# TensorE's loop body turned by part of a tile, and its code aligned to blocks of 256 instructions, in a linear-attention layer

## Chip, core and metric

One Trainium2 chip, one core of it. The metric is the device time of one execution in microseconds (us), as the median of runs; smaller is better.

## What is computed

A layer with causal linear attention and a feed-forward part, on x of 8 sequences x 2048 positions x 512 values, 16 heads of 32, in float32:

```python
q = split_heads(x @ Wq.T + bq); k = split_heads(x @ Wk.T + bk); v = split_heads(x @ Wv.T + bv)
q, k = exp(q), exp(k)
kv = cumsum(k[:, :, :, None] * v[:, :, None, :], axis=1)
k1 = cumsum(k, axis=1)
num = einsum('zsD,zsDd->zsd', q, kv)
den = sum(q * k1, axis=-1, keepdims=True)
x = layernorm(x + merge_heads(num / den) @ Wo.T + bo)
x = layernorm(x + tanh(x @ weight @ aux_weight1 @ aux_weight2 + bias))
```

## The kernel before

The work is cut into 128 tiles of 128 positions, tile n being positions 128 (n // 8) onward of sequence n % 8. For a tile the kernel works out the scores within it, masks them, multiplies by V ("attend"), adds what a running state of the earlier tiles gives, divides by the denominators, projects with Wo, normalises, and multiplies by Wf, the product of the three feed-forward matrices, made once at the start.

Each engine has its own program, written out by hand, and they meet only by semaphores. The unit is `slot(c, k)`, the work of one step, k from 0 to 7 in a chunk of 8 tiles. `run_slots` (L213) writes the first slots out, then a loop of 13 iterations of 8 slots (`nc.Fori`, L219, with `hint_back_edge=True`), then the last slots. The first and last slots know their number when the program is built (`c.static()`); those in the loop compare semaphores with registers that five instructions set at the top of each iteration (L181 to L183). The loop's branch is a compare-and-branch at the end, and a hint instruction at the top names it.

On TensorE a slot has two parts. Small matmuls, five groups of 16 float32 instructions, which the chip runs as 32 weight loads and 32 matmuls each: denominators of tile k-1 (L368), the state's share of its numerator (L372), scores of tile k (L425), attend of k-1 (L381), the state's update by k-2 (L436). Then large ones, of 12 weight loads and 12 matmuls with 512 columns each: Q's and K's projections for tile k+4, V's for k, the output projection of k-1 and the feed-forward of k-2, all by `three_pass` (L309; its three matmuls are L312, L313, L314). A load and a matmul are an instruction each. Waits on semaphores are carried by a load or, where there is more than one, stand as instructions of their own: 13 in a slot (two before the denominators, three before scores, one before attend, two before Q, one before K, two before the output projection, two before the feed-forward). A slot so is 453 instructions: 13 and 440 loads and matmuls. With the hint, five register instructions, the addition and the branch the loop's body is 3632.

The other engines' parts (ScalarE evicts and exponentiates, VectorE scans, divides and normalises, GpSimd masks and splits in two parts, SyncE loads and stores) are not touched.

Of the kernel before, what the change touches and what calls it, by code (L numbers as in the profile page):

```python
# [26 lines left out]
def linear_attention_ffn_kernel(nc, x, wqT, wkT, wvT, woT, bq, bk, bv, bo, w, a1T, a2, bf, out):  # L27
# [5 lines left out]
    P = 128  # L33
    B, S, D = x.shape
    NK = D // P
    HD = 32
    HG = P // HD
    QUAD = 4
    NI = S // P
    NT = NI * B  # L40
# [16 lines left out]
    with ctx:  # L57
# [106 lines left out]
        def wait(engine, semaphore, value):  # L164

            if not isinstance(value, int) or value > 0:
                engine.wait_ge(semaphore, value)

        def wait_before(engine, *waits):

            engine.wait_ge(mhalf_ready, 1)
            for semaphore, value in waits:
                wait(engine, semaphore, value)
# [134 lines left out]
        def _(pe):  # L308
# [37 lines left out]
                pe.wait_ge(c_ready, 1)  # L346
                pe.wait_ge(consts_ready, 1)

            def slot(c, k):
                b = k % QUAD  # L350
                s = (k // QUAD) % 2
                ns = 1 - s
                cols = slice(b * P, (b + 1) * P)
                att = c.exists(k)
                prev = c.exists(k - 1)
                ffn = c.exists(k - 2)
                proj = c.exists(k + 4)
                heads = [(g, j, slice(g * HD, (g + 1) * HD), slice(j * HD, (j + 1) * HD))
                         for g in range(NK) for j in range(HG)]

                def denominators(n):

                    ts, tcols = (n // QUAD) % 2, slice(n % QUAD * P, (n % QUAD + 1) * P)

                    wait_before(pe, (qk1_ready, c.count(n + 1)), (o_ready, c.count(n)),
                                (state_ready, c.state_count(n - 1)))
                    for g, j, quarter, h in heads:
                        last = nc.tensor.matmul(den_ps[quarter, j, :], ones[h, :], qk1[h, g, :], start=True, stop=True)  # L368
                    last.then_inc(den_done, 1)
                    if c.reads_state(n):  # L370
                        for g, j, quarter, h in heads:
                            nc.tensor.matmul(num_ps[quarter, j, :], state[h, n % B, g, :], QT[h, ts, g, tcols],  # L372
                                             start=True, stop=False, skip_group_check=True)

                def attend(n):
                    wait(pe, v_ready, c.count(n + 1))
                    wait(pe, masked, c.count(n + 1))
                    for j in range(HG):
                        for g in range(NK):
                            f0 = g * P + j * HD  # L380
                            last = nc.tensor.matmul(num_ps[g * HD:(g + 1) * HD, j, :], V[:, n % 2, f0:f0 + HD],  # L381
                                                    A[:, n % 2, j, g, :], start=not c.reads_state(n),
                                                    stop=True, skip_group_check=True)
                    last.then_inc(num_done, 1)

                def output_projection():
                    if not ffn:
                        pe.wait_ge(woh_ready, 1)
                        pe.wait_ge(wol_ready, 1)
                    wait(pe, oh_ready, c.count(k))  # L390
                    wait(pe, ol_ready, c.count(k))

                    if att:
                        wait(pe, scores_out[3], c.count(k + 1))
                    wait(pe, r_ready, c.count(k - 1))
                    three_pass(oproj_ps, lambda f: oH[:, f, :], lambda f: oL[:, f, :],
                               lambda f: WoH[:, f, :], lambda f: WoL[:, f, :]).then_inc(oproj_done, 1)

                def feed_forward():
                    wait(pe, x1h_ready, c.count(k - 1))  # L400
                    wait(pe, x1l_ready, c.count(k - 1))

                    if proj:
                        wait(pe, q_ready, c.count(k + 5))
                    elif att:
                        wait(pe, scores_out[0], c.count(k + 1))
                    wait(pe, z_ready, c.count(k - 2))
                    three_pass(ffn_ps, lambda f: x1H[:, f, :], lambda f: x1L[:, f, :],
                               lambda f: WfH[:, f, :], lambda f: WfL[:, f, :]).then_inc(ffn_done, 1)

                if att and prev:
                    denominators(k - 1)
                if att:
                    wait(pe, k_ready, c.quad_count(k))
                    wait(pe, q_ready, c.quad_count(k))

                    wait(pe, z_ready, c.count(k - 2))
                    wait(pe, k_ready, c.count(k + 4))
                    wait(pe, v_ready, c.count(k))  # L420
                    wait(pe, r_ready, c.count(k - 1))
                    if not prev:
                        pe.wait_ge(c_ready, 1)
                    for g, j, _, h in heads:
                        last = nc.tensor.matmul(SC[:, j, g * P:(g + 1) * P], KT[h, s, g, cols],  # L425
                                                QT[h, s, g, cols], start=True, stop=True)
                    last.then_inc(scores_done, 1)
                if att and prev:
                    attend(k - 1)
                if c.updates_state(k - 2):  # L430
                    n = k - 2
                    wait(pe, ktok_loaded[n % B], c.part_count(n))
                    for g in range(NK):
                        for j in range(HG):
                            f0 = g * P + j * HD
                            last = nc.tensor.matmul(state_ps[j * HD:(j + 1) * HD, g * HD:(g + 1) * HD],  # L436
                                                    Ktok[:, j * P + g * HD:j * P + (g + 1) * HD],
                                                    V[:, n % 2, f0:f0 + HD], start=True, stop=True)
                    last.then_inc(state_done, 1)
                if proj:  # L440
                    if not c.exists(k + 3):
                        pe.wait_ge(wqh_ready, 1)
                        pe.wait_ge(wql_ready, 1)
                    wait(pe, xh_ready, c.quad_count(k + 4))
                    wait(pe, xl_ready, c.quad_count(k + 4))

                    if att:
                        wait(pe, scores_out[0], c.count(k + 1))
                    wait(pe, q_ready, c.count(k + 4))
                    three_pass(qproj_ps, lambda f: WqH[:, f, b * P:(b + 1) * P],  # L450
                               lambda f: WqL[:, f, b * P:(b + 1) * P], lambda f: xTH[:, ns, f, :],
                               lambda f: xTL[:, ns, f, :]).then_inc(qproj_done, 1)
                    if not c.exists(k + 3):
                        pe.wait_ge(wkh_ready, 1)
                        pe.wait_ge(wkl_ready, 1)
                    if att:
                        wait(pe, scores_out[1], c.count(k + 1))
                    wait(pe, k_ready, c.count(k + 4))
                    three_pass(kproj_ps, lambda f: WkH[:, f, b * P:(b + 1) * P],
                               lambda f: WkL[:, f, b * P:(b + 1) * P], lambda f: xTH[:, ns, f, :],  # L460
                               lambda f: xTL[:, ns, f, :]).then_inc(kproj_done, 1)
                if att:
                    if not prev:
                        pe.wait_ge(wvh_ready, 1)
                        pe.wait_ge(wvl_ready, 1)
                    wait(pe, scores_out[2], c.count(k + 1))
                    three_pass(v_ps, lambda f: xTH[:, s, f, cols], lambda f: xTL[:, s, f, cols],
                               lambda f: WvH[:, f, :], lambda f: WvL[:, f, :]).then_inc(v_done, 1)
                if att and not c.exists(k + 1):
                    denominators(k)  # L470
                    attend(k)
                if prev:
                    output_projection()
                if ffn:
                    feed_forward()

            run_slots(pe, slot, 8, 2, {-3: multiply_aux, -2: multiply_weight, -1: multiply_bv})

        @block.scalar
        def _(act):  # L480
# [355 lines left out]
```

## Time and profile before

| what | value |
|---|---|
| median of 3 runs | 2352.6 us (2350.2 to 2352.68) |
| the profiled execution's own time | 2354.96 us |
| its span, first to last instruction | 2353.2 us |
| granted TensorE clock, mean | 0.991 |
| TensorE busy (matmuls) | 2250.8 us, 96% |
| TensorE weight loads | 1833.2 us, 78% |
| VectorE, GpSimd, ScalarE busy | 1620.6, 1289.1, 1012.5 us |
| instruction queue q8 | 235 packets, 3.85 MB |

### The profile page before, as it was taken

The page shows a single profiled execution, that of the slowest core. Times are in us where ns is not written, and L with a number is a line of the kernel's source. Part 1 is how long each engine was busy: PE and PEld are TensorE (multiplying, and loading weights), DVE is VectorE, ACT ScalarE, POOL GpSimd, SP SyncE. Part 2 cuts the span into 40 slices and gives each one's busy share as a digit, 9 for nine tenths or more (in the row PEclk, how much of TensorE's full clock was granted, in tenths as well). Part 3 has the DMA queues.
Part 4 walks back from the last instruction along what each step waited for, and adds up shares of the span by engine and source line. Part 5 has one row for each costly group of instructions (what it writes and reads, how often), then busy time and mean ns, then how long its engine had stood idle before and what let it go on. Part 6 is the DMA issues. An engine that isn't in the chain of part 4 may idle for free.

```text
span 2353.2 us, 71216 instructions
## 1 busy us (share of the span) xinstructions
PE 2250.8 (96%) x27784; PEld 1833.2 (78%) x27784; DVE 1620.6 (69%) x2444; ACT 1012.5 (43%) x1683; POOL 1289.1 (55%) x1797
## 2 busy tenths in 40 slices
PE   3999999999999999999999999999999999999985
PEld 2778887878888888887878788787888878788864
DVE  3477776776776767767767767677777677677674
ACT  2344444444444444444444444444444444444442
POOL 1255555556555555555555555555555655555553
PEclk9999999999999999999999999999999999999997
DMA  5133333333333333333333333333333333333221
GB/s 156 46 101 107 108 108 107 104 108 109 105 110 103 109 109 104 109 108 100 113 105 105 105 107 109 104 105 107 110 104 109 109 100 107 111 101 113 69 68 55
DMA packets 294453, 242.74 MB, mean 103 GB/s; under 512 B 33329, under 2 KB 225841, under 8 KB 294193
## 3 DMA queue, kind: packets, MB, share of 16 engines
q1 hardware_dynamic: 294192, 238.69, 32.5%
q8 instruction: 235, 3.85, 0.7%
q14 instruction: 26, 0.20, 0.0%
HBM read 139.99 MB, written 98.57 MB: 101 GB/s over the span
## 4 chain that ended last, share of the span: by engine, by line
PE 94%; issue 2%; DVE 2%; ACT 1%; DMA 1%; POOL 1%; SPq 0%; POOLq 0%; DVEq 0%; ACTq 0%
PE SC L312 26%; PE SC L313 25%; PE SC L314 24%; PE SC L425 6%; PE ND L381 5%; PE ND L372 3%; PE ND L368 2%; PE ND L436 2%; DVE o L670 0%; PE ND L312 0%; PE ND L313 0%; PE ND L314 0%; DMA KT<-wkT 0%; DMA QT<-wqT 0%; ACT A L552 0%
## 5 line engine op out<-in xcount | busy, mean ns | idle before, releaser
L756 POOL TENSOR_SCALAR_AFFINE_SELECT A<-A 128x512 f32<-128x512 f32 x512 | 327.8, 674 | 313.2 <-ACT A L552 313.1
L670 DVE RECIPROCAL o<-ND 128x512 f32<-128x512 f32 x128 | 427.8, 3342 | 1.1 <-PE ND L381 0.9
L727 DVE TENSOR_TENSOR xres<-SC,xres 128x512 f32<-128x512 f32 x128 | 88.6, 692 | 457.0 <-PE SC L314 456.8
L750 POOL TENSOR_TENSOR oL<-o,oH 128x512 fp32r<-128x512 f32 x128 | 166.1, 1298 | 324.8 <-ACT oH L531 324.8
L542 ACT ACTIVATE WK<-xres,shift,rstd 128x512 f32<-128x512 f32 x128 | 104.4, 816 | 530.4 <-POOL shift L796 530.4
L552 ACT ACTIVATE A<-SC 128x512 f32<-128x512 f32 x512 | 264.7, 603 | 48.7 <-PE SC L425 48.6
L312 PE MATMUL SC<-xTH,WqH 128*128 128x512 f32 x512 | 211.3, 413 | 31.4 <-POOL xTL L785 27.3
L785 POOL TENSOR_TENSOR xTL<-xin,xTH 128x512 fp32r<-128x512 f32 x128 | 165.7, 1295 | 100.8 <-ACT xTH L580 100.7
L312 PE MATMUL SC<-WfH,x1H 128*128 128x512 f32 x512 | 201.4, 393 | 14.4 <-issue 7.8
L683 DVE TENSOR_TENSOR_SCAN WK<-ones,k,KT 128x128 f32<-128x128 f32 x512 | 207.7, 468 | 9.9 <-PE ND L368 9.9
L313 PE MATMUL SC<-xTL,WqH 128*128 128x512 f32 x512 | 201.2, 393 | 13.0 <-issue 13.0
L557 ACT ACTIVATE QT<-SC,bcol 128x512 f32<-128x512 f32 x128 | 88.4, 691 | 289.8 <-PE SC L314 289.8
L312 PE MATMUL SC<-WoH,oH 128*128 128x512 f32 x512 | 201.0, 393 | 9.8 <-issue 7.8
L312 PE MATMUL SC<-xTH,WkH 128*128 128x512 f32 x512 | 200.3, 391 | 7.7 <-DVE WkL L616 7.7
L312 PE MATMUL SC<-WvH,xTH 128*128 128x512 f32 x512 | 199.6, 390 | 2.7 <-ACT A L552 2.7
L314 PE MATMUL SC<-xTH,WqL 128*128 128x512 f32 x512 | 201.4, 393 | 0.0
L313 PE MATMUL SC<-WfL,x1H 128*128 128x512 f32 x512 | 200.8, 392 | 0.0
L314 PE MATMUL SC<-WfH,x1L 128*128 128x512 f32 x512 | 200.5, 392 | 0.0
L314 PE MATMUL SC<-WoH,oL 128*128 128x512 f32 x512 | 200.4, 391 | 0.0
L313 PE MATMUL SC<-WoL,oH 128*128 128x512 f32 x512 | 200.2, 391 | 0.0
L313 PE MATMUL SC<-xTL,WkH 128*128 128x512 f32 x512 | 200.0, 391 | 0.0
L314 PE MATMUL SC<-xTH,WkL 128*128 128x512 f32 x512 | 199.9, 390 | 0.0
(100 smaller groups left out, 5025.0 us busy)
## 6 DMA issues: line engine op xcount, KB each, us to landing
xin<-x SPq DMA_DIRECT2D x512, 64.0 KB, 1.8
xres<-x SPq DMA_DIRECT2D x128, 256.0 KB, 2.6
x_rows<-WK SPq DMA_DIRECT2D x128, 256.0 KB, 2.9
WK<-x_rows SPq DMA_DIRECT2D x512, 64.0 KB, 2.0
out<-WK SPq DMA_DIRECT2D x128, 256.0 KB, 2.1
k_rows<-WK SPq DMA_DIRECT2D x120, 256.0 KB, 2.0
WK<-k_rows SPq DMA_DIRECT2D x480, 64.0 KB, 1.9
QT<-wqT SPq DMA_DIRECT2D x4, 256.0 KB, 4.5
```

Of the source, the lines that this page charges most:

```text
L312: nc.tensor.matmul(out, statH(k), movH(k), start=(k == 0), stop=False)
L313: nc.tensor.matmul(out, statH(k), movL(k), start=False, stop=False)
L314: last = nc.tensor.matmul(out, statL(k), movH(k), start=False, stop=(k == NK - 1))
L381: last = nc.tensor.matmul(num_ps[g * HD:(g + 1) * HD, j, :], V[:, n % 2, f0:f0 + HD], A[:, n % 2, j, g, :], start=not c.reads_state(n), st ...
L425: last = nc.tensor.matmul(SC[:, j, g * P:(g + 1) * P], KT[h, s, g, cols], QT[h, s, g, cols], start=True, stop=True)
L542: nc.scalar.activation(x1[:, n % 2, :], xres[:, n % 2, :], ACT.Identity, bias=shift[:, 0:1], scale=rstd[:, 0:1]).then_inc(x1_ready, 1)
L552: nc.scalar.activation(A[:, k % 2, j, :, :].rearrange("p g q -> p (g q)"), SC[:, j, :], ACT.Copy).then_inc(scores_out[j], 1)
L670: nc.vector.reciprocal(o[:, :, :], den_ps).then_inc(recip_ready, 1)
L683: last = nc.vector.tensor_tensor_scan(qk1[:, g, :], ones[:, 0:1].to_broadcast([P, P]), KT[:, s, g, cols], k1[:, k % B, g:g + 1], ALU.mult, ...
L750: nc.gpsimd.tensor_tensor(oL[:, :, :], o[:, :, :], oH[:, :, :].bitcast(F32), ALU.subtract).then_inc(ol_ready, 1)
L756: last = nc.gpsimd.affine_select(out=A[:, k % 2, j, :, :], in_=A[:, k % 2, j, :, :], compare_op=ALU.is_ge, fill=0.0, base=0, pattern=[[0, ...
L785: nc.gpsimd.tensor_tensor(halves[1], xin[:, m % XIN, :].rearrange("p (t g q) -> p g t q", t=HG, q=HD), halves[0].bitcast(F32), ALU.subtrac ...
```

## The change

`slot` is cut in two: `small(c, k)` with the small matmuls and `large(c, k)` with the projections. The order of all matmuls stays as it was. What moves is the place where the loop begins and ends: an iteration was small(0), large(0), ..., small(7), large(7), and is now large(0), small(1), large(1), ..., large(7), small(8), with the first `small` in front of the loop. Two directives on the places of instructions are new. `head_slot={pe.engine: 160}` puts the loop's first instruction at place 160 of a block of 256. `addr_align(256, offset=0, max_nops=255)` in front of V's projection fills up with no-operation instructions until V's first load is the first of a block: 39 behind the loop's head (160 + 57 instructions = 217), and 59 in the seven other tiles (453 + 59 = 512). It is written in the loop alone. The last alignment is followed by 404 instructions, the branch among them, so the loop ends 148 instructions into a block.

```diff
+            def small(c, k):
...
                 if att and prev:
-                    denominators(k - 1)
+                    denominators(c, k - 1)
...
+            def large(c, k):
...
+                if not c.static():
+
+                    pe.addr_align(256, offset=0, max_nops=255)
                 if att:
                     if not prev:
                         pe.wait_ge(wvh_ready, 1)
...
-            run_slots(pe, slot, 8, 2, {-3: multiply_aux, -2: multiply_weight, -1: multiply_bv})
+            setup = {-3: multiply_aux, -2: multiply_weight, -1: multiply_bv}
+            for t in range(-8, B):
+                small(Chunk(t // B), t % B)
+                large(Chunk(t // B), t % B)
+                if t in setup:
+                    setup[t]()
+
+            small(Chunk(1), 0)
+            with nc.Fori(1, NI - 2, engines=(pe.engine,), hint_back_edge=True, head_slot={pe.engine: 160}) as it:
+                c = Chunk(it, pe)
+                for k in range(B):
+                    large(c, k)
+                    small(c, k + 1)
+            for t in range(NT - 2 * B, NT + 2):
+                if t > NT - 2 * B:
+                    small(Chunk(t // B), t % B)
+                large(Chunk(t // B), t % B)
```

On TensorE, the loop's head in the kernel before, from the entry on (ISA rows are the register instructions):

```order
L219 UNCONDITIONAL_BRANCH
L219 BRANCH_PREFETCH_HINT
L219 ISA
L181 ISA x3
L183 ISA
L368 MATMUL ND<-WK,ones 32x128 x16
L372 MATMUL ND<-QT,state 32x128 x16
L425 MATMUL SC<-QT,KT 128x128 x16
L381 MATMUL ND<-A,V 32x128 x16
L436 MATMUL ND<-V,WK 32x32 x16
L312 MATMUL SC<-xTH,WqH 128x512
```

and in the changed kernel, where the small matmuls have other line numbers (L359, L363, L398, L372 and L409 for L368, L372, L425, L381 and L436), and the ISA row of L498 ahead of the branch is the directive for place 160:

```order
L372 MATMUL ND<-A,V 32x128 x16
L409 MATMUL ND<-V,WK 32x32 x16
L498 ISA
L498 UNCONDITIONAL_BRANCH
L498 BRANCH_PREFETCH_HINT
L498 ISA
L181 ISA x3
L183 ISA
L312 MATMUL SC<-xTH,WqH 128x512
L313 MATMUL SC<-xTL,WqH 128x512
```

The five small groups have gone in front of the loop, and Q's projection is what follows the registers. The loop's end on TensorE in the kernel before:

```order
L312 MATMUL SC<-WfH,x1H 128x512
L313 MATMUL SC<-WfL,x1H 128x512
L314 MATMUL SC<-WfH,x1L 128x512
L219 REGISTER_ALU
L219 COMPARE_AND_BRANCH
```

and in the changed kernel:

```order
L314 MATMUL SC<-WfH,x1L 128x512
L359 MATMUL ND<-WK,ones 32x128 x16
L363 MATMUL ND<-QT,state 32x128 x16
L398 MATMUL SC<-QT,KT 128x128 x16
L372 MATMUL ND<-A,V 32x128 x16
L409 MATMUL ND<-V,WK 32x32 x16
L498 REGISTER_ALU
L498 COMPARE_AND_BRANCH
```

The branch stood behind the feed-forward's long matmuls and now stands behind the state's update. The seam between K's and V's projection on TensorE in the changed kernel:

```order
L313 MATMUL SC<-xTL,WkH 128x512
L314 MATMUL SC<-xTH,WkL 128x512
L474 ISA
L312 MATMUL SC<-WvH,xTH 128x512
L313 MATMUL SC<-WvL,xTH 128x512
```

The ISA row is the directive that becomes 39 or 59 no-operations; in the kernel before the row of WkL is followed by that of WvH at once.

## Rows read from the trace of the kernel before

**Rows 1.** The page: busy times, and the chain that ended last.

```profile
PE 2250.8 (96%) x27784; PEld 1833.2 (78%) x27784; DVE 1620.6 (69%) x2444; ACT 1012.5 (43%) x1683; POOL 1289.1 (55%) x1797
PE 94%; issue 2%; DVE 2%; ACT 1%; DMA 1%; POOL 1%; SPq 0%; POOLq 0%; DVEq 0%; ACTq 0%
PE SC L312 26%; PE SC L313 25%; PE SC L314 24%; PE SC L425 6%; PE ND L381 5%; PE ND L372 3%; PE ND L368 2%; PE ND L436 2%; DVE o L670 0%; PE ND L312 0%; PE ND L313 0%; PE ND L314 0%; DMA KT<-wkT 0%; DMA QT<-wqT 0%; ACT A L552 0%
```

**Rows 2.** Waits of TensorE in 219:2038.5: total us, times, longest us.

```profile
PE SC L313 <- issue: 13.0, 12, 1.5
PE ND L436 <- issue: 2.7, 9, 0.4
PE ND L372 <- issue: 1.5, 5, 0.4
```

**Rows 3.** Timeline of weight loads behind one return: start us, us, instruction, [idle before].

```profile
1059.51 0.23 PEld L368 LDWEIGHTS ND<-WK,ones 32*32 32x32 f32 x32 [0.35 <-issue]
1059.64 0.43 PEld L372 LDWEIGHTS ND<-QT,state 32*32 32x32 f32 x5
1060.78 0.23 PEld L372 LDWEIGHTS ND<-QT,state 32*32 32x32 f32 x27 [0.70 <-issue]
...
1063.73 0.19 PEld L313 LDWEIGHTS SC<-xTL,WqH 128*128 128x128 f32 x1
1065.36 0.19 PEld L314 LDWEIGHTS SC<-xTH,WqL 128*128 128x128 f32 x1 [1.44 <-issue]
...
1078.86 0.23 PEld L368 LDWEIGHTS ND<-WK,ones 32*32 32x32 f32 x32 [0.35 <-issue]
```

**Rows 4.** Queue q8 in 1057.3:1057.5, 1062.9:1063.0, 1066.8:1066.9 and 1056:1196: packets, MB, share.

```profile
q8 instruction: 1, 0.02, 61.2%
q8 instruction: 1, 0.02, 60.0%
q8 instruction: 1, 0.02, 77.2%
q8 instruction: 15, 0.25, 0.8%
```

**Rows 5.** The same timeline in the iteration before that.

```profile
920.64 0.23 PEld L372 LDWEIGHTS ND<-QT,state 32*32 32x32 f32 x27 [0.29 <-issue]
...
924.67 0.19 PEld L314 LDWEIGHTS SC<-xTH,WqL 128*128 128x128 f32 x1 [0.89 <-issue]
```

**Rows 6.** Timelines of a clean tile: weight loads, Q's first matmul, the next tile's start.

```profile
1096.10 0.23 PEld L368 LDWEIGHTS ND<-WK,ones 32*32 32x32 f32 x32 [0.35 <-issue]
1096.24 0.66 PEld L372 LDWEIGHTS ND<-QT,state 32*32 32x32 f32 x32
1097.10 0.99 PEld L425 LDWEIGHTS SC<-QT,KT 32*128 32x128 f32 x32 [0.20 <-issue]
1098.21 0.81 PEld L381 LDWEIGHTS ND<-A,V 128*32 128x32 f32 x32
...
1099.55 0.47 PE L312 MATMUL SC<-xTH,WqH 128*128 128x512 f32 x1
...
1113.32 0.23 PEld L368 LDWEIGHTS ND<-WK,ones 32*32 32x32 f32 x32 [0.35 <-issue]
```

**Rows 7.** Timeline of weight loads: first tile of the loop, first tile behind it.

```profile
222.35 0.23 PEld L368 LDWEIGHTS ND<-WK,ones 32*32 32x32 f32 x32 [0.35 <-issue]
...
2041.51 0.18 PEld L368 LDWEIGHTS ND<-WK,ones 32*32 32x32 f32 x16 [0.35 <-issue]
2042.25 0.16 PEld L368 LDWEIGHTS ND<-WK,ones 32*32 32x32 f32 x13 [0.56 <-issue]
```

**Rows 8.** Queue q8 in 2038.5:2040.5, behind the loop's end.

```profile
q8 instruction: 1, 0.02, 3.0%
```

**Rows 9.** Timeline of matmuls: three gaps of the last tiles.

```profile
2261.38 0.47 PE L312 MATMUL SC<-WoH,oH 128*128 128x512 f32 x1 [2.60 <-issue]
2278.15 0.47 PE L312 MATMUL SC<-WoH,oH 128*128 128x512 f32 x1 [2.60 <-issue]
2293.51 0.76 PE L312 MATMUL SC<-WoH,oH 128*128 128x512 f32 x1 [2.60 <-issue]
```

**Rows 10.** Windows around them: us, PE busy (instructions), granted clock, DMA share, GB/s.

```profile
2262.60:2266.00 3.40, 3.40 (x10) 0.51 0.22 82
...
2275.40:2278.20 2.80, 0.20 (x2) 1.00 0.36 103
2278.20:2285.00 6.80, 6.79 (x88) 1.00 0.10 39
...
2293.40:2296.80 3.40, 3.29 (x8) 0.50 0.00 0
```

More of the change, by code:

```diff
@@ L347, in multiply_bv, with denominators @@
                 pe.wait_ge(consts_ready, 1)
-            def slot(c, k):
+            heads = [(g, j, slice(g * HD, (g + 1) * HD), slice(j * HD, (j + 1) * HD))
+                     for g in range(NK) for j in range(HG)]
+            def denominators(c, n):
+                ts, tcols = (n // QUAD) % 2, slice(n % QUAD * P, (n % QUAD + 1) * P)
+                wait_before(pe, (qk1_ready, c.count(n + 1)), (o_ready, c.count(n)),
+                            (state_ready, c.state_count(n - 1)))
+                for g, j, quarter, h in heads:
+                    last = nc.tensor.matmul(den_ps[quarter, j, :], ones[h, :], qk1[h, g, :], start=True, stop=True)
+                last.then_inc(den_done, 1)
+                if c.reads_state(n):
+                    for g, j, quarter, h in heads:
+                        nc.tensor.matmul(num_ps[quarter, j, :], state[h, n % B, g, :], QT[h, ts, g, tcols],
+                                         start=True, stop=False, skip_group_check=True)
@@ new lines, in attend @@
+            def attend(c, n):
+                wait(pe, v_ready, c.count(n + 1))
+                wait(pe, masked, c.count(n + 1))
+                for j in range(HG):
+                    for g in range(NK):
+                        f0 = g * P + j * HD
+                        last = nc.tensor.matmul(num_ps[g * HD:(g + 1) * HD, j, :], V[:, n % 2, f0:f0 + HD],
+                                                A[:, n % 2, j, g, :], start=not c.reads_state(n),
+                                                stop=True, skip_group_check=True)
+                last.then_inc(num_done, 1)
@@ new lines, in small @@
+            def small(c, k):
+                s = (k // QUAD) % 2
+                cols = slice(k % QUAD * P, (k % QUAD + 1) * P)
+                att = c.exists(k)
+                prev = c.exists(k - 1)
+                if att and prev:
+                    denominators(c, k - 1)
+                if att:
+                    wait(pe, k_ready, c.quad_count(k))
+                    wait(pe, q_ready, c.quad_count(k))
+                    wait(pe, z_ready, c.count(k - 2))
+                    wait(pe, k_ready, c.count(k + 4))
+                    wait(pe, v_ready, c.count(k))
+                    wait(pe, r_ready, c.count(k - 1))
+                    if not prev:
+                        pe.wait_ge(c_ready, 1)
+                    for g, j, _, h in heads:
+                        last = nc.tensor.matmul(SC[:, j, g * P:(g + 1) * P], KT[h, s, g, cols],
+                                                QT[h, s, g, cols], start=True, stop=True)
+                    last.then_inc(scores_done, 1)
+                if att and prev:
+                    attend(c, k - 1)
+                if c.updates_state(k - 2):
+                    n = k - 2
+                    wait(pe, ktok_loaded[n % B], c.part_count(n))
+                    for g in range(NK):
+                        for j in range(HG):
+                            f0 = g * P + j * HD
+                            last = nc.tensor.matmul(state_ps[j * HD:(j + 1) * HD, g * HD:(g + 1) * HD],
+                                                    Ktok[:, j * P + g * HD:j * P + (g + 1) * HD],
+                                                    V[:, n % 2, f0:f0 + HD], start=True, stop=True)
+                    last.then_inc(state_done, 1)
@@ L357, in slot @@
                 proj = c.exists(k + 4)
[L358 to L384, printed above, removed]
                 def output_projection():
@@ L409, in feed_forward @@
                                lambda f: WfH[:, f, :], lambda f: WfL[:, f, :]).then_inc(ffn_done, 1)
-                if att and prev:
-                    denominators(k - 1)
[L414 to L439, printed above, removed]
                 if proj:
@@ L469, in slot @@
                 if att and not c.exists(k + 1):
-                    denominators(k)
-                    attend(k)
+                    denominators(c, k)
+                    attend(c, k)
                 if prev:
```

## Prediction

> **What bounds the kernel now.** I read the page first. TensorE is busy 96% of the span and is 94% of the chain that ended last, nearly all on the three lines of the projections and the five of the small matmuls [rows 1]. VectorE, the next, is at 69%. So time comes and goes only as TensorE's stream gets denser or thinner. Next I asked what TensorE waited for in the stretch of the loop, 219 to 2038.5 us. It waits for no other engine there: all its idle time ends with "issue", 12 times before L313, up to 1.5 us each, and 14 shorter ones before L436 and L372 [rows 2]. The reader is to see that the tile's data is always there and that something in the delivery of instructions is late, about once for each of the 12 returns to the loop's head.
>
> Then the timeline of the weight loads around one return. The five small groups start at 1059.51; the fifth load of L372 is followed by 0.70 us of nothing (resumed 1060.78), and the second load of the Q projection by 1.44 us (resumed 1065.36) [rows 3]. I counted the instructions between the two resumptions, each float32 matmul of 16 being 32 loads and 32 matmuls, and each further wait an instruction of its own: the matmul of the fifth load 1, the other 27 pairs 54, three semaphore waits 3, scores 64, one wait 1, attend 64, state 64, two waits 2, the first pair of Q 2, the next load 1. That is 256, the number that the change aligns to. The instruction queue q8 began one packet of 0.02 MB in 1057.3 to 1057.5, one in 1062.9 to 1063.0 and one in 1066.8 to 1066.9, and 15 in the whole iteration [rows 4], whose body is 3632 instructions (14.2 blocks). So a block is asked for when the one ahead of it is entered, one block ahead only, and takes 1065.36 - 1060.78 = **4.58 us** to be usable; in another iteration 924.67 - 920.64 = 4.03 us [rows 5]. It shows only where 256 instructions run out faster, and a tile's 320 small ones take 3.45 us (1096.10 to 1099.55 in a clean tile, whose 60 large matmuls have the other 13.8 us, 0.23 us each) [rows 6]. The Trainium skill ("Runtime: NRT & Kernel Launch", Instruction fetch mechanics) says that crossing a 16 KiB boundary is mostly hidden; by that the change would have nothing to win. The row of 1.44 us differs, and decides.
>
> **What alignment removes.** A clean tile lasts 1113.32 - 1096.10 = 17.22 us, or 17.24 us; the first tile of this iteration 1078.86 - 1059.51 = 19.35 us [rows 3, 6]. From the first L368 load of the loop (222.35) to the one behind it (2041.51) are 1819.16 us for 104 tiles [rows 7]. At 17.23 us they would be 1791.9 us: **27 us** is all that late blocks cost in the loop. In the new order a tile is 453 instructions and a pad of 59, so two blocks: V, O and FFN, 36 pairs at 0.23 us (8.3 us), are in front of the small ones, and the next boundary falls 47 instructions into scores; behind it are some 2.2 us of small ones and 5.5 us of Q and K. Both stretches exceed 4.58 us. I take the whole 27 us as gone.
>
 In the kernel before that request comes a whole projection phase ahead of the branch. In the new one it comes in scores. The sequencer has just waited there, so it enters the last block between the first load of scores (1097.10) and the moment the array reaches that instruction, 47/64 of 1.11 us later (1097.9); I take 1097.3. Small matmuls end and Q begins at 1099.55 [rows 6]. The request takes between 3.8 us (1.4 us from the resumption at 1065.36 to the next packet, and 2.4 us from the packet begun at 1062.9 to 1063.0 to its use at 1065.36) [rows 3, 4] and 4.58 us; I take 4.2, between them. Behind the jump come the branch, the hint, five register instructions and two waits before Q's first load. No row prices those; three waits before scores leave 0.30 us (0.20 idle and a load's 0.10) [rows 6], so 0.10 each, about 1.0 us in all. They were free before, under the queued FFN; behind the small matmuls nothing is queued. Q then starts at 1097.3 + 4.2 + 1.0 = 1102.5 instead of 1099.55: **+2.95 us** at each of 12 returns, 35 us. Bounds: 1097.3 + 3.8 + 0.8 gives +2.35 (28 us), 1097.9 + 4.58 + 1.0 gives +3.9 (47 us). The Trainium skill, same section, says that a branch to a target outside the two pages held forces a fetch before execution goes on; with the measured 4 us it speaks against the new place, and the trace agrees as to the exit.
>
> The next block after the jump (V's) is asked for at the jump and needed 1.0 + 24 x 0.23 = 6.5 us later: hidden. Entering the loop costs one such jump, 0 to 3 us; the tiles outside the loop stay unaligned, and those behind it will meet their boundaries at other places than before (0.56 us at the exit is one). I take +1 us for both, within -2 to +4.
>
> **The clock.** Each return leaves TensorE idle for about 3 us. Three gaps of that size stand in the tail: 2.60 us idle before 2261.38, and two like it; the granted clock was then 0.51 for 3.4 us (2262.6 to 2266.0) and 0.50 (2293.4 to 2296.8), and stayed 1.00 after the one at 2275.4 [rows 9, 10]. That is 2.4 GHz down to 1.2, and costs 1.7 us each time. In the loop the array was busier before the gap than there, so I count half of 12 returns: +10 us, bounds 0 and 20 us.
>
> **What the pads cost.** 91 pads of 59 instructions and 13 of 39 stand between K's last matmul and V's first. They hide if they end within the sequencer's lead. That lead from rows: after the jump the packet of the following block began at 1057.3 to 1057.5, a request precedes its packet by 1.4 us (above), and the array came to the first small load at 1059.51 [rows 3, 4]: 3.5 us. So up to 3.5/59 = 59 ns each costs nothing. Below, a load or matmul passes in 3.6 ns (L368: 64 in 0.23 us) [rows 6]; above, a semaphore wait takes 0.10 us. No row shows a pad. It waits for nothing and sets nothing, so I put it under the wait, at 59 ns or less, and price 0. At 0.10 us it is (5.9 - 3.5) x 91 = +218 us. The Trainium skill ("TensorE: Matmul & The Clock Gate", Wait — 56ns, not 53.3ns?) gives about 62 ns for a matmul decoded in software; were a pad the same, the sum would be +14 us more.
>
> **Sum.** -27 + 35 + 1 + 10 = +19 us. The profiled execution took 2354.96 us beside its span of 2353.2, 2.4 us above the median of 2352.6, so the forecast is 2352.6 + 19 to 21: **2373 us**. Its own range is -27 + 28 - 2 = -1 to -27 + 47 + 4 + 20 = +44: 2352 to 2397.
>
> **Rivals.**
> - *The head is there in time* (faster). If it is asked for earlier than at entry to the last block, or is kept, only the 1.0 us of branch, registers and waits shows: -27 + 12 + 1 = -14 us, 2339; with these hidden too, 2326. It decides once a return costs under 27/12 = 2.25 us, and my low bound is 2.35. For it: the branch of before shows no idle time. Against it: 15 packets an iteration, one for each block, so nothing is kept, and the exit.
> - *The pads show* (slower). V's matmuls start late in every tile by 59 times the pad's price less 3.5 us. From 59 ns up, each 10 ns adds 54 us; at 0.07 to 0.10 us the time is 2430 to 2590. For it: every instruction of the sequencer that a row shows costs 0.10 us. Against it: a pad has nothing to wait for.
> - *The change doesn't do what it says.* If the blocks don't begin where the padding assumes, the stalls of before remain at other tiles, and the new loop end is cheap or dear by luck: about 2353.
>
> **How the numbers follow.** Return stall with hidden pads 0.43, of which 0.03 within 0.2% (4.7 us, about what a measurement of this kernel can tell from no change); head in time 0.27, nearly all faster; pads show 0.24; no effect 0.06, split mostly into the same. Faster 0.28, same 0.08, slower 0.64. The range takes the likeliest case, the faster one and the lower edge of the pads: 2328 to 2440 us. The likeliest one's own is 2352 to 2397.
>
> **What would show it.** Right: no idle time at L372 and L313 in the loop, clean tiles of 17.2 us, seven in eight; one gap of about 3 us before the first L312 of Q at each of 12 returns; 17 q8 packets an iteration; some short stretches at half clock behind the gaps. If the pads show, the gap stands before the first L312 of V (WvH) in each tile. I am wrong if the gap before Q is under 2 us, or if tiles stay at 19 us somewhere in the body.

## The result, and the profile after

The changed kernel takes **2416.95 us** (median of 6 runs, 2412.0 to 2420.73) against 2352.41 us of the kernel before on the same chip (6 runs, 2350.2 to 2352.68): ratio 1.0278, 95% interval 1.0264 to 1.0292. It is 64.5 us slower, where +21 us was forecast. The direction held. The wide range, 2328 to 2440 us, held too, because it took in the lower edge of the rival "The pads show"; the range of the likeliest case alone, 2352 to 2397 us, did not. Most of the excess is one term.

The page of the changed kernel, lines that answer to [rows 1], and the groups of the first matmul of Q's and of V's projection (busy us, mean ns of one, idle time before them). The last line is V's group in the kernel before:

```profile
PE 2277.1 (94%) x27752; PEld 1832.2 (76%) x27752; DVE 1613.9 (67%) x2444; ACT 1010.8 (42%) x1683; POOL 1287.4 (53%) x1797
q8 instruction: 261, 4.28, 0.9%
PE 92%; issue 3%; DVE 2%; ACT 1%; DMA 1%; POOL 1%; SPq 0%; POOLq 0%; DVEq 0%; ACTq 0%
L312 PE MATMUL SC<-xTH,WqH 128*128 128x512 f32 x512 | 215.0, 420 | 67.4 <-issue 36.3
L312 PE MATMUL SC<-WvH,xTH 128*128 128x512 f32 x512 | 207.0, 404 | 21.7 <-issue 19.0
L312 PE MATMUL SC<-WvH,xTH 128*128 128x512 f32 x512 | 199.6, 390 | 2.7 <-ACT A L552 2.7
```

TensorE still bounds the kernel. "issue" rose from 2% to 3% of the chain, and V's projection, which had no wait that ended with "issue" before, has 19.0 us of them. The loop's waits of TensorE (219 to 2120 us; total us, times, longest), beside [rows 2]:

```profile
PE SC L312 <- issue: 55.2, 104, 3.2
PE SC L398 <- issue: 2.4, 2, 1.9
```

The waits that stood at L313, L436 and L372 of the kernel before are gone: in the aligned loop no block of instructions is late inside the body. In their place L312 waits once in every tile of the loop: 91 times before V, 12 times before Q at the returns and once before Q at the entry. (The wait at the exit is in the row of L398.) The timeline of weight loads shows the two places. Around a return to the loop's head, beside [rows 3]:

```profile
1237.70 0.23 PEld L359 LDWEIGHTS ND<-WK,ones 32*32 32x32 f32 x32 [0.35 <-issue]
...
1240.60 0.47 PEld L409 LDWEIGHTS ND<-V,WK 128*32 128x32 f32 x32
1244.32 0.19 PEld L312 LDWEIGHTS SC<-xTH,WqH 128*128 128x128 f32 x1 [3.25 <-issue]
...
1245.36 0.20 PEld L314 LDWEIGHTS SC<-xTH,WqL 128*128 128x128 f32 x1
1245.67 0.33 PEld L312 LDWEIGHTS SC<-xTH,WqH 128*128 128x128 f32 x1
...
1248.23 0.33 PEld L312 LDWEIGHTS SC<-xTH,WkH 128*128 128x128 f32 x1
...
1259.75 0.23 PEld L359 LDWEIGHTS ND<-WK,ones 32*32 32x32 f32 x32 [0.35 <-issue]
```

Q's matmuls begin 6.65 us behind the tile's start here and 6.27 us in the mean of the 12 returns (5.81 to 6.65), 3.45 us in a clean tile [rows 6]. From 1245.67 the loads last 0.33 us and stand 0.43 us apart, not 0.23: the array runs at its lower clock level. Windows over that stretch and the next (us, busy times with instructions of PE, PEld, DVE, ACT, POOL, granted clock, DMA share, GB/s):

```profile
1245.60:1249.00 3.40, 3.40 (x9) 2.65 (x8) 2.08 (x5) 0.11 (x1) 0.00 (x0) 0.51 0.34 98
1249.00:1254.00 5.00, 5.00 (x24) 4.13 (x22) 0.71 (x2) 2.31 (x4) 3.48 (x5) 1.00 0.45 134
```

Queue q8 in 1099:1243.4, one iteration, and in 1240.1:1240.3:

```profile
q8 instruction: 17, 0.28, 1.0%
q8 instruction: 1, 0.02, 57.2%
```

Seventeen packets for 17 blocks, and the packet of the loop's head begins 2.5 us behind the tile's start at 1237.70 (1.2 us for the entry to the last block, and the 1.4 us that a request precedes its packet, would give 2.6). In the other seven tiles of an iteration the gap stands between K's and V's projection. Timeline of matmuls, and the next two tile starts among the weight loads:

```profile
1268.28 0.39 PE L313 MATMUL SC<-xTL,WkH 128*128 128x512 f32 x1
1268.50 0.39 PE L314 MATMUL SC<-xTH,WkL 128*128 128x512 f32 x1
1269.11 0.47 PE L312 MATMUL SC<-WvH,xTH 128*128 128x512 f32 x1 [0.21 <-issue]
1269.41 0.39 PE L313 MATMUL SC<-WvL,xTH 128*128 128x512 f32 x1
1269.64 0.40 PE L314 MATMUL SC<-WvH,xTL 128*128 128x512 f32 x1
...
1277.46 0.23 PEld L359 LDWEIGHTS ND<-WK,ones 32*32 32x32 f32 x32 [0.35 <-issue]
```

The reader is to look at the starts, not at the [0.21]: each row is drawn 0.39 us long though the next starts after 0.23 us, so they overlap, and the idle time understates the loss. Starts are 0.23 us apart in the stream, but 0.61 and then 0.30 us around V's first. That is 0.38 + 0.07 = 0.45 us, and the tile lasts 1277.46 - 1259.75 = 17.71 us against 17.23. Times 91 such tiles, 43.7 us.

What the sequencer does (the part of the engine that takes the instructions in order and hands loads and matmuls to the array) isn't among these rows. Its own records in the trace, which I counted:

```
changed kernel     pads: 5876 (91 x 59 + 13 x 39), 75.2 ns from one to the next;
                   V's first matmul 0.07 us behind the last pad, 4.43 us behind the first
                   branch to the loop's head: 1.55 to 2.39 us long in 12 returns
                   (kernel before: 0.34 to 0.40 us)
```

**The sum, measured.** From the first tile's start to the last's, 2270.7 us against 2206.7, +64.0. Pads 91 x 0.48 = +43.7; returns 12 x (6.27 - 3.45) = +33.8; lower clock in 5 of the 12, 1.6 us each (Q's projection 4.3 us in place of 2.8, and K's first matmuls), +8.1; late blocks in the body gone, -27; the tile behind the entry 21.66 us, +4.4; the tile at the exit 20.71 in place of 19.02, +1.7; the tiles behind it, -1.0. Together +63.7.

### The profile page after: what moved, and what is told of

The parts are those of the page before. It is cut to its first block, busy times and chain, and to the rows that moved or that the text cites. A ratio compares the mean times of both kernels' runs of the same rounds, so it can differ in the third digit from the quotient of the medians.

```text
span 2416.3 us, 77029 instructions
## 1 busy us (share of the span) xinstructions
PE 2277.1 (94%) x27752; PEld 1832.2 (76%) x27752; DVE 1613.9 (67%) x2444; ACT 1010.8 (42%) x1683; POOL 1287.4 (53%) x1797
## 4 chain that ended last, share of the span: by engine, by line
PE 92%; issue 3%; DVE 2%; ACT 1%; DMA 1%; POOL 1%; SPq 0%; POOLq 0%; DVEq 0%; ACTq 0%
PE SC L312 26%; PE SC L314 24%; PE SC L313 24%; PE SC L398 6%; PE ND L372 5%; PE ND L363 3%; PE ND L359 2%; PE ND L409 1%; DVE o L699 0%; PE ND L312 0%; PE ND L313 0%; PE ND L314 0%; DMA QT<-wqT 0%; DMA KT<-wkT 0%; ACT A L581 0%
## 5 line engine op out<-in xcount | busy, mean ns | idle before, releaser
L312 PE MATMUL SC<-xTH,WqH 128*128 128x512 f32 x512 | 215.0, 420 | 67.4 <-issue 36.3
L312 PE MATMUL SC<-WvH,xTH 128*128 128x512 f32 x512 | 207.0, 404 | 21.7 <-issue 19.0
L312 PE MATMUL SC<-WfH,x1H 128*128 128x512 f32 x512 | 201.1, 393 | 14.4 <-issue 7.9
L312 PE MATMUL SC<-WoH,oH 128*128 128x512 f32 x512 | 201.1, 393 | 9.7 <-issue 7.8
L312 PE MATMUL SC<-xTH,WkH 128*128 128x512 f32 x512 | 200.8, 392 | 7.4 <-DVE WkL L645 7.4
L313 PE MATMUL SC<-xTL,WqH 128*128 128x512 f32 x512 | 205.0, 400 | 0.0
L313 PE MATMUL SC<-WoL,oH 128*128 128x512 f32 x512 | 200.5, 392 | 0.0
L313 PE MATMUL SC<-WfL,x1H 128*128 128x512 f32 x512 | 200.4, 391 | 0.0
L314 PE MATMUL SC<-WvH,xTL 128*128 128x512 f32 x512 | 200.1, 391 | 0.0
L313 PE MATMUL SC<-WvL,xTH 128*128 128x512 f32 x512 | 200.1, 391 | 0.0
```

The costliest lines, as they stand in the source:

```text
L312: nc.tensor.matmul(out, statH(k), movH(k), start=(k == 0), stop=False)
L313: nc.tensor.matmul(out, statH(k), movL(k), start=False, stop=False)
L314: last = nc.tensor.matmul(out, statL(k), movH(k), start=False, stop=(k == NK - 1))
```

## The experiments

Theory 1: what the forecast lacked is the pads' price; take them out of the sequencer's way and the rest of the forecast stands, some 2373 us. Theory 2: the new loop end costs more than its 35 + 10 us. Further runs then asked what the loop end needs in order to cost nothing. The kernel before ran beside each, at 2350.1 to 2352.6 us; where runs are compared with each other closely, it is by their distance from it.

**1. A branch over the pads.** With `max_nops=0` the same alignment is made by a branch over the gap.

```diff
-                    pe.addr_align(256, offset=0, max_nops=255)
+                    pe.addr_align(256, offset=0, max_nops=0)
```

> The changed kernel with max_nops=0 in V's alignment: a branch in place of 59 (or 39) no-operations, same blocks, same loop. Theory 1 (pads: 59 at 75 ns are 4.4 us, longer than the 4.1 us for which the array is supplied ahead, 0.48 us a tile, 91 tiles, 44 us): V's gap goes if the branch costs under 4 us, and the time falls by about 44 us to 2373. Theory 2 (V's block itself arrives late at the boundary, or crossing into it costs 0.4 us): the gap before V stays near 0.38 us and the time stays within 5 us of 2417. A third outcome: the taken branch waits for its block, and V's gap grows.

Measured 2376.13 us (2374.48 to 2377.75), ratio 1.0104 (1.0089 to 1.0118): 40.8 us less than the changed kernel. Every tile of the loop but those at the returns lasts 17.2 us, and the same waits as above read

```profile
PE SC L312 <- issue: 36.4, 14, 3.2
PE SC L398 <- issue: 2.1, 2, 1.6
```

14 waits in place of 104: the entry, the 12 returns, and one of 0.2 us behind the exit. The 91 gaps before V are gone. Theory 1 holds.

**2. The pads in two parts.** In each of the 91 tiles 29 stand ahead of K's waits and 30 ahead of V, so that K's projection lies between them.

```diff
+                    if not c.static():
+                        pe.addr_align(256, offset=201, max_nops=255)
```

> The changed kernel with a second alignment, at place 201, ahead of K's projection: 29 of the 59 pads stand there and 30 ahead of V; V still begins a block, nothing else moves. Theory 1 (pads outlast the supply of 4.1 us): 30 pads are 2.3 us and hide, tiles return to 17.23 us, 2373 us. Theory 2 (the boundary at V is the cost): no change, 2417 us. The return stall of 2.9 us and the half clock behind it stay in both.

Measured 2374.76 us (2372.05 to 2376.33), ratio 1.0095 (1.008 to 1.011). Waits:

```profile
PE SC L312 <- issue: 36.4, 14, 3.4
```

All the pads are there, and cost nothing: what costs is 59 in one run. This is a second confirmation, and the base of the next two.

**3. The seam of before, with aligned blocks.** Run 2 with the loop as small(0), large(0), ... again, so that the branch is behind the feed-forward's matmuls, 78 instructions into its block.

```diff
-            small(Chunk(1), 0)
-            with nc.Fori(... head_slot={pe.engine: 160}) as it:
+            with nc.Fori(... head_slot={pe.engine: 78}) as it:
...
+                    small(c, k)
                     large(c, k)
-                    small(c, k + 1)
```

> As e2, but the loop begins with the small matmuls and ends with the feed-forward as in the kernel before (head at place 78 of a block). The return then stands 76 instructions into V's block, so the head is asked for some 8 us ahead of the branch, and the branch and register instructions lie under the queued feed-forward. Theory 1 (the return costs 2.9 us because the last block is entered just ahead of the branch, plus half clock behind it, 12 times; unaligned code cost 27 us): 2352.4 - 27 = 2326 us, no gap at the return. Rival (any aligned loop pays the return, since blocks are held nowhere): 2365 to 2373.

Measured 2346.63 us (12 runs, 2336.03 to 2353.89), ratio 0.9976 (0.9963 to 0.999). The expected 2326 was missed. The body itself is clean; the returns are not. Timeline of loads at one of them:

```profile
1203.00 0.19 PEld L314 LDWEIGHTS SC<-WfH,x1L 128*128 128x128 f32 x1
1205.07 0.25 PEld L359 LDWEIGHTS ND<-WK,ones 32*32 32x32 f32 x29 [1.88 <-issue]
```

1.88 us in place of 0.35. In the trace's records the branch took 3.36 to 3.90 us in 8 of the 12 returns and the head's packet began 0.6 us behind it; in the other 4 it had begun 1.8 to 4.8 us ahead and the branch took 0.45 to 0.56 us. A late return costs 1.9 to 2.7 us over its two tiles at full clock, a second wait of up to 0.6 us following in scores, and 5.5 us in the two that the lower clock followed: 24.5 us in the profiled execution of 2353.9 us, so that 2329 us would be left. A branch behind long matmuls is no warrant that its target is there: the head's packet must begin ahead of it, and here it mostly did not.

**4. The loop begins with V's projection.** V, output projection, feed-forward, the small groups, then Q and K of the next tile; the branch stands behind K's long matmuls.

```diff
+            large(Chunk(1), 0, ('qk',))
...
+            with nc.Fori(... head_slot={pe.engine: 0}) as it:
...
+                    large(c, k, ('vof',), align=k > 0)
                     small(c, k + 1)
+                    large(c, k + 1, ('qk',))
```

> As e2, but the loop begins with V's projection (head at place 0) and ends with K's: the last block is entered in scores, some 7 us ahead of the branch, and V, output projection and feed-forward (8.3 us) follow the jump. Theory 1: no gap at the return, 2326 us, like e3. Rival (the return costs about the same wherever it stands): 2365 to 2373.

Measured 2332.46 us (2329.59 to 2333.09), ratio 0.9914 (0.9901 to 0.9926). Every tile of the loop is 17.2 us, returns included, and the branch takes 0.35 us. What is left is at the exit, above all this wait:

```profile
2031.69 0.50 PE L313 MATMUL SC<-WoL,oH 128*128 128x512 f32 x1 [2.63 <-issue]
```

**5. Nine and fifty pads.** The split at place 181 in place of 201, to find how many pads in one run hide.

> As e2 (2375 us), but 9 of the 59 pads ahead of K and 50 ahead of V. The pads run 75 ns apart, so 50 are 3.76 us. If the array is supplied for 4.1 us when K's last matmul has been issued (what the changed kernel's gap says: 59 pads 4.44 us, gap 0.38 us), they hide and the time is e2's, within 3 us. If the supply is the 3.5 us of the prediction, each tile shows 0.3 us and more, and the time is 30 us above e2.

Measured 2600.6 us (2597.11 to 2602.21), ratio 1.1065 (1.1046 to 1.1083). This was an oversight of mine: the iteration's first K projection comes at place 192, past 181, so that the directive filled up to the next block's 181, 245 pads once in each of 13 iterations. Matmuls at one of them:

```profile
1201.44 0.76 PE L312 MATMUL SC<-xTH,WkH 128*128 128x512 f32 x1 [13.96 <-issue]
```

245 x 75 ns = 18.4 us less the 4 us of lead is 14.4. (The lead is the time by which the sequencer is ahead of the array when it comes to the pads.) The other tiles are 17.24 us with 50 pads ahead of V; the total says nothing on that, so it was run again as 11.

**6. The new seam alone.** The changed kernel without V's alignment.

> The changed kernel without the alignment ahead of V: the body is turned and its head stands at place 160, no pads at all. The last block is then entered 208 instructions ahead of the branch, in the small matmuls. Theory 1: the return still shows, as the rest of the request (4.2 us less some 2.8) and 1.0 us of branch and registers, less than in e2, about 2 us, 12 times, and unaligned tiles stay: 2365 to 2385 us. Rival (alignment, not the seam, made the return dear): near 2352.

Measured 2371.0 us (2367.89 to 2376.78), ratio 1.0096 (1.0077 to 1.0114). With this seam, alignment without pads gains nothing: run 1 is 23.6 us above its kernel before, this run 20.9. Both branches lie behind the small groups. Return tiles are 18.65 to 21.94 us here. Summed from the traces, the late blocks of the body cost 6 us here and under 1 in run 1, but the 12 return tiles cost 32.5 us over clean ones here and 43.8 in run 1, whose last block is entered only 148 instructions ahead of the loop's end, in place of some 208.

**7. The old seam, the last block 32 places earlier.** Run 3 with V at place 32, K at 233, head at 110: the branch is 110 instructions into its block.

```diff
...
-                    pe.addr_align(256, offset=0, max_nops=255)
+                    pe.addr_align(256, offset=32, max_nops=255)
...
```

> e3 with every block boundary 32 instructions earlier (V begins at place 32, K at 233, the head at 110): the last block is entered in K's last instructions, with the pads ahead of V still behind it, instead of at V's first. In e3 8 of 12 returns waited 3.4 to 3.9 us for the head, whose packet began only 0.6 us behind the branch, while in the other 4 it had begun ahead of it. If the head's request needs more time between the entry of the last block and the branch than V, output projection and feed-forward give, this version has it ready every time: 2326 to 2332 us. If not time but something else makes the request miss, returns keep waiting: 2340 to 2350.

Measured 2329.17 us (2328.36 to 2330.1), ratio 0.9914 (0.9897 to 0.993). The head's packet begins 6 us ahead of the branch in all 12 returns; the first tile behind them lasts 17.2 to 17.6 us.

**8. V first, with an aligned tail.** Run 4, with the code behind the loop put at a block's start and aligned too.

```diff
...
+            pe.addr_align(256, offset=0, max_nops=0)
```

> e4 (2332.5 us) with the code behind the loop aligned too: a branch to the next block at the exit, under K's queued matmuls, and pads as in the loop up to tile 121. In e4 the exit leaves a gap of 2.6 us ahead of L313 and the tiles behind it lose about 1 us. Theory: the exit's fetch hides under the 4.1 us of supply, 2329 us. Rival: the exit's branch waits about as long as the crossing did, 2332 us.

Measured 2328.09 us (2326.78 to 2329.86), ratio 0.9909 (0.9892 to 0.9925). That is 22.0 us under the kernel before, where run 4 was 20.1 under its own; the intervals of the two ratios overlap, so the total doesn't show the gain. The exit tile does: 19.72 us in place of 21.86.

**9 and 10. Where the last block begins.** Run 3 with V at place 4 (K 205, head 82, the branch 82 instructions in and four pads at the block's start), and at place 254 (K 199, head 76).

> e3 with every boundary 4 instructions earlier: the last block's first instructions are four of the 30 pads, V's first load is its fifth. In e3, where the last block begins with V's first load behind a pad, the head was asked for ahead of the branch in only 4 of 12 iterations; in e7, 32 earlier, in all 12. If what counts is that the last instruction of the block before is a pad, this one misses like e3, 2340 to 2350 us; if the distance to the branch counts, it should be no better than e3 either, since 4 places change little. A hit in all 12 returns would speak against both and for the kind of the block's first instruction.

> e3 with every boundary 2 instructions later: V's first load and matmul end one block, its second load begins the last one, so no pad touches the boundary. If a pad just ahead of the boundary makes the head's request miss, all 12 returns have it in time and the branch takes 0.35 us: 2326 to 2332 us. If the distance from the last block's entry to the branch counts, it misses like e3 or more: 2340 to 2355 us.

One run each, beside before at 2352.19 us: V at 4 takes 2324.91 us, V at 254 2343.36 us. With V at 4 all 12 returns have the head in time (packet 4.7 to 5.3 us ahead), every tile of the loop is 17.22 to 17.24 us, and the loop's waits of TensorE hold no "issue" at all:

```profile
PE SC L398 <- DVE WK L706: 1.8, 1, 1.8
PE SC L312 <- ACT A L581: 1.0, 1, 1.0
```

With V at 254, 7 of 12 returns missed, with 3.2 to 3.8 us in the branch. That pads at the block's start help and a matmul's load at its start does not was one reading of run 9; run 12 tried it.

**11. Nine and fifty pads, mended.** Run 5 with K's alignment left out in the iteration's first tile.

```diff
-                    if not c.static():
+                    if not c.static() and k > 0:
```

> e5 mended. There K's alignment to place 181 met the loop's first tile at place 193 and put 244 pads in it once in an iteration, which made its 2600 us; the seven other tiles showed 17.24 us with 50 pads ahead of V. Here the first tile has no alignment ahead of K and 39 pads ahead of V, as in the changed kernel. 50 pads at 75 ns are 3.76 us: with a supply of 4.1 us they hide, and the time is e2's 2375 us within 4 us; with a supply of 3.5 us, the prediction's, it would be some 30 us more.

Measured 2379.18 us (2375.67 to 2382.04), ratio 1.0114 (1.009 to 1.0138). The tiles with 50 pads are 17.24 us: 50 x 75 = 3.75 us hide, 59 x 75 = 4.4 us do not, which with the gap of 0.38 us puts the lead at 3.75 to 4.1 us. (The first tile's fill in run 5 was 245 pads from place 192 by the trace, not 244 from 193.) The 4.4 us above run 2, just outside the 4 us expected, stand at the returns: the same 14 waits, but

```profile
PE SC L312 <- issue: 40.2, 14, 3.4
```

and 8 stretches at the lower clock in place of 6. Why the returns wait 0.3 us longer there is open.

**12. The old seam, V at 0, the branch at 82.** Run 3 with four of the pads in front of the feed-forward, so that the block begins with V's load as in run 3, and the branch is 82 instructions in as in run 9 (K at 205, head at 82). By the trace the four come from those ahead of V, 26 in place of 30, and not from the 29 ahead of K.

```diff
...
+                if not c.static():
+                    pe.addr_align(256, offset=54, max_nops=255)
...
```

> The old seam with aligned blocks as in the run of 2346.6 us, V's projection at place 0 of its block and so still beginning that block with its weight load. Four of the pads stand ahead of the feed-forward matmuls instead of K's projection, so that the branch back lies 82 instructions into its block, as in the run of 2324.9 us, in place of 78. Theory A, the number of instructions between the last block's beginning and the branch decides whether the loop head is there in time (78 and 76 missed in 8 and 7 of 12 returns, 82 and 110 in none): all 12 returns have it, branch at 0.35 to 0.6 us, 2325 to 2330 us. Theory B, what stands at the block's first places decides (pads in the run that always had it, a matmul's weight load in the one that missed): misses in half or more of the returns with 3 to 4 us in the branch, 2338 to 2354 us.

Measured 2328.57 us (2327.56 to 2329.31), ratio 0.9901 (0.9883 to 0.9919). All 12 returns had the head:

```
run   branch at   returns with the head late   branch, us      head's packet from the branch, us
 10      76             7 of 12                3.17 to 3.79    +0.6; the 5 others -4.9 to -2.0
  3      78             8 of 12                3.36 to 3.90    +0.6; the 4 others -4.8 to -1.8
 12      82             0                      0.44 to 0.48    -5.2 to -4.4
  9      82             0                      0.34 to 0.45    -5.3 to -4.7
  7     110             0                      0.33 to 0.38    -6.6 to -5.8
```

What stands at the block's start is ruled out; how far behind it the branch lies decides, between 78 and 82 instructions here. It is not that the request had too little time: the last pad ahead of V stands 5.9 to 6.1 us ahead of the branch in run 3, in the late returns as in the others, which is more than the 4.6 us that a request took from entry to use in the kernel before, and 6.2 us in run 12, and the head's packet begins either 1.8 to 5 us ahead of the branch or only 0.6 us behind its start. Four pads are also 0.3 us and shift the entry to the block by as much, so whether instructions or time decide, and what does it, is open.

## Why the prediction was wrong by 44 us

**The step that failed** is the pads' price: "It waits for nothing and sets nothing, so I put it under the wait, at 59 ns or less, and price 0". A pad takes 75 ns, and 59 of them in one run outlast the lead by 0.38 us. No row of before showed a pad; between ends of 3.6 ns and 0.10 us I chose below the threshold by an argument from what a pad doesn't do, where the nearer rows were those of the sequencer's other instructions. The lower end was no price of the sequencer at all: [rows 6] show when 64 loads and matmuls began on the array, and the sequencer, some 3.5 us ahead by [rows 3, 4], had handed them over before. Run 1 gives their cost, 40.8 us, and run 2 the mechanism: the same pads in two parts are free. The rival "The pads show" had the place and the mechanism right, and too high a cost: "from 59 ns up, each 10 ns adds 54 us" would make 86 us at 75 ns. The other mis-sized term is the lead: it is 4.05 us (4.43 less the 0.38 that V is late), not 3.5, so the threshold is 69 ns. The Trainium skill ("TensorE: Matmul & The Clock Gate", Wait — 56ns, not 53.3ns?) gives about 62 ns for a matmul decoded in software; the pad measured here is above that too.

**What held.** Runs 1 and 2 are the forecast's own likeliest case with hidden pads, and measured 2376.1 and 2374.8 us against 2373.
- *Alignment removes 27 us*: the body's waits at L313, L436 and L372 are gone, 17 packets an iteration came. The whole 27 us is seen in run 9, 2352.2 to 2324.9, one execution; its trace has 1792.0 us from the loop's first tile to the one behind the loop, where [rows 7] have 1819.16.
- *The return, +2.95 us*: +2.82 in the mean, 33.8 us for 35. The request at entry to the last block fits the packets 2.3 to 2.5 us behind the tile's start, and from the branch's end to Q's first load are 0.90 us, for 1.0. (The loop ends 148 instructions behind the boundary, not the 146 of the prediction; nothing hangs on the two.) The rule of the Trainium skill ("Runtime: NRT & Kernel Launch", Instruction fetch mechanics), that a branch outside the pages held forces a fetch first, agrees with branches of 1.55 to 2.39 us there.
- *The clock, 6 of 12 at 1.7 us, +10*: 5 of 12 at 1.6 us, +8. Granted clock 0.51, that is 1.2 GHz, for 3.4 us behind a gap of 3 us, as in the tail of before. That it was half of the returns was a guess that came near.

**What was small and off.** Entry and tail were put at +1 us within -2 to +4; they cost 4.4 + 1.7 = 6.1, and with the tiles behind the exit, 1.0 us shorter, 5.1. The entry is a return's stall in full with the lower clock on top, where I allowed 0 to 3 us. The rival "The head is there in time" is false for this seam, but true of other loop ends: runs 4, 7, 9 and 12.

## What to carry to other kernels

Aligning an engine's code to its blocks is worth what late blocks cost, here 27 us of 2352; but both the filling and the loop's end must be laid out. Put no more no-operations in one run than the engine's lead covers (50 here, at 75 ns each), spread them between long instructions or branch over them, and count out where each directive falls, since a place that is already passed costs up to a whole block of them. Let the branch back stand behind long work and far enough into its block (82 instructions held, 78 did not), and measure a seam before believing that its target is there.

Where a price is known only from both sides of a threshold and each 10 ns beyond it is worth tens of microseconds, it is the term to weigh by both branches, not by a story about why it ought to be cheap.

## What the runs showed of the hardware that was not expected

- A no-operation on TensorE takes 75 ns to pass the sequencer (5876 of them in the changed kernel; 245 in a row left 14 us of idle time in run 5), and only the sequencer's own records show them. Up to 50 in a row hid under the lead (run 11), 59 did not.
- The loop's head was late in 8 and 7 of 12 returns with the branch 78 and 76 instructions into its block and in none at 82, though 82 and 78 differ by 0.3 us. The head's packet began 0.6 us behind the branch or 1.8 to 5 us ahead of it, with nothing between: an either-or, not a slope. It also differed from one return to the next of the same execution; run 3's 12 times, whose loop has such returns, are spread over 18 us, the 4 of run 12 over 2. Why is open.
- Half clock did not follow every gap of 3 us: 5 of 12 in the changed kernel, 6 in runs 1 and 2, 8 in run 11. What decides it was not tried.
